# Attention with q/k pieces made a turn earlier, the output weights loaded behind the last transpose, and VectorE's low half behind its maximum

## The chip, the cores and the metric

The kernel runs on one core of a Trainium2 chip. The metric is device time of one launch in microseconds. Five engines matter: TensorE (PE, matmuls into PSUM), VectorE (DVE), ScalarE (ACT), GpSimd (POOL) and SyncE (SP, which here only issues DMAs). They run side by side, each in the order of its own program, and wait for each other by semaphores.

## The reference, cut to what matters

The program has two layers, each an attention times a gate from a mixture of experts. The change touches only the first layer's attention, over 1024 tokens of width 256, with 16 heads of 128:

```python
q = jnp.einsum('bse,ehd->bshd', x, wq)
k = jnp.einsum('bse,ehd->bshd', x, wk)
v = jnp.einsum('bse,ehd->bshd', x, wv)
qn = rms_norm(q, q_scale)
kn = rms_norm(k, k_scale)
scores = jnp.einsum('bqhd,bkhd->bhqk', qn, kn)
attn = jax.nn.softmax(scores, axis=-1)
out = jnp.einsum('bhqk,bkhd->bqhd', attn, v)
return jnp.einsum('bqhd,hde->bqe', out, wo)
```

## The kernel before

A turn t is one head; in it stand eight steps m, one for each tile of 128 queries against all 1024 keys. Every matmul operand is kept as a high and a low f16 half, so each product is three matmuls. The order on every engine is written out by hand; there is no scheduler.

One tile goes through these instructions. TensorE makes its scores into two of four PSUM banks (L1102 to L1106). VectorE takes the negated row maximum from PSUM (`a_nmax`, L1237). ScalarE takes the exponential into one of two buffers `a_ex`, with the row sum in an accumulator that a second instruction reads out (L1180). VectorE makes the scale of the rows from the sum (`a_part`, `a_share`, L1241 and L1243; called share here). ScalarE writes the scaled high half (`a_halves`, L934), VectorE the low half (L940). SP transposes both by DMA (L949) into `a_pT`, and TensorE multiplies with v (L1118 to L1120, called values). There are three `a_halves` buffers, so a high half also waits for the transpose three tiles back.

The waits of the exponential decide much here. `exps(t, m)` waits for its maximum and for the low half of tile m - 2, which is the last reader of the buffer that it writes:

```python
u, past = (t, m - 2) if m >= 2 else (t - 1, QT + m - 2)
wait_low(act, u, past)
```

In step m, TensorE makes the scores of tile m + 2, a side piece, and a quarter of the values. ScalarE takes the exponential of tile m + 1, copies the side pieces out of PSUM, and writes the high half of tile m + 1. VectorE's step is: low half of tile m, share of m + 1, maximum of m + 2, side work.

The ten side pieces prepare the coming heads. Pieces 0 to 3 are q and k (two token tiles each, L1088 to L1090; ScalarE copies out the squares, L1159, and the value, L1160), 4 and 5 are v (ScalarE's high half L1171, VectorE's low half L1230), 6 to 9 are transposes of the normalised q and k (L1075, ScalarE L1166, VectorE L1225). They take turns in two PSUM banks, so that a piece waits until the piece two before it is copied out, with its low half where it has one. `MADE` says which piece of which head stands in which step. Between q/k and their transposes stands the norm, in two halves: VectorE sums the squares (`squares`, L1210 and L1213), GpSimd takes the power (L1026) and multiplies q and k (L1029). GpSimd also splits the weights of coming heads (L712 to L716) and weights of later stages (L801 to L805).

At the end, `wo_halves` (two tiles of 1 MB that lie over `sq` and `qk`) are loaded, and the next stage's `project` (L1857 to L1859) multiplies the heads' outputs with them, head by head.

Of the kernel before, what the change touches and what calls it, by code (L numbers as in the profile page):

```python
# [16 lines left out]
D = 256  # L17
# [6 lines left out]
H, HD = 16, 128  # L24
# [790 lines left out]
def attention0(nc, env, w):  # L815

    sem, psum, ident = env["sem"], env["psum"], env["ident"]
# [2 lines left out]
            ("turn", 0, 0), ("turn", 1, 0), ("turn", 0, 1), ("turn", 1, 1)]  # L820
    NS, QK, TURN_FIRST = len(SIDE), 4, 6

    MADE = {0: (1, (3,)), 1: (1, (6,)), 2: (1, (7, 4)), 3: (1, (8,)), 4: (1, (9, 5)),
            5: (2, (0,)), 6: (2, (1,)), 7: (2, (2,))}
    VALUES = {5: (0, 0, 0), 6: (0, 0, 1), 7: (0, 0, 2), 0: (1, 0, 3), 1: (1, 1, 0), 2: (1, 1, 1), 3: (1, 1, 2), 4: (1, 1, 3)}
    OUT_AT = {2: 0, 6: 1}
    VB, PB = 3, 3
# [9 lines left out]
    def coming(t, ahead):  # L837

        return not fixed(t) or t + ahead < H

    FIRST = [("side", 0, s) for s in range(NS)] + [("side", 1, s) for s in range(3)]

    def units(t):

        if fixed(t) and t < 0:
            return FIRST
        made = []
        for m in range(QT):
            ahead, sides = MADE[m]
            if coming(t, ahead):  # L850
                made += [("side", ahead, s) for s in sides]
        return made

    def has_low(unit):
# [18 lines left out]
    def unit_count(t, unit):  # L873
        return first_unit(t) + units(t).index(unit) + 1
# [9 lines left out]
    with ExitStack() as local:  # L884
# [9 lines left out]
        later = SplitWeights(nc, env, w, tmp)  # L894
# [4 lines left out]
        total, part, share = (tmp(n, [P, QT]) for n in ("total", "part", "share"))  # L899
# [2 lines left out]
        halves = [tmp(f"halves{b}", [P, KT, 2, P], F16) for b in range(PB)]  # L902

        scale_loaded = [sem(f"a0_sld{b}") for b in range(2)]
        wo_loaded = sem("a0_wol")
        turned = [sem(f"a0_tu{b}") for b in range(PB)]
        (scale_ready, made, high_done, low_done, ss_ready, var_ready, pow_ready, r_ready, qkn_ready, s_ready, max_ready,
         exp_ready, part_ready, share_ready, p_high, p_low, pv_ready, o_high, o_low) = (
# [9 lines left out]
            return psum[:, at:at + 2, :].rearrange("p a b -> p (a b)")  # L918

        def sides_at(t, m):  # L920
            ahead, sides = MADE[m]
            return [("side", ahead, s) for s in sides] if coming(t, ahead) else []

        def wait_low(engine, t, m):

# [11 lines left out]
        def tile_low(dve, t, m):  # L937
            i = QT * t + m
            dve.wait_ge(p_high, i + 1)
            dve.scalar_tensor_tensor(halves[i % PB][:, :, 1, :], ex[m % 2][:, :].rearrange("p (k q) -> p k q", q=P),  # L940
                                     share[:, m:m + 1], halves[i % PB][:, :, 0, :], ALU.mult, ALU.subtract).then_inc(p_low, 1)
# [33 lines left out]
        with nc.Block() as block:  # L975
            @block.sync
            def _(sp):
                def load(h):
                    sp.wait_ge(w_ready, h - 1)
                    weights.load(sp, h, h % 2)  # L980

                for i, name in enumerate(("L0_attn_q_scale", "L0_attn_k_scale")):
                    sp.dma_start(scales[:, i:i + 1], w[name].rearrange("(p a) -> p a", a=1)).then_inc(scale_loaded[i], 16)
                load(2)
                for k in range(2):
                    later.load(sp, k)
                for t in range(H):
                    turn_tile(sp, t, 0)
                    if t + 3 < H:
                        load(t + 3)  # L990
                    turn_tile(sp, t, 1)
                    if t > 0:
                        later.store(sp, t - 1)
                    if 0 < t < later.CHUNKS - 1:
                        later.load(sp, t + 1)
                    turn_tile(sp, t, 2)
                    if t == H - 1:
                        sp.wait_ge(ss_ready, 2 * H)
                        sp.wait_ge(made, unit_count(H - 2, ("side", 1, NS - 1)))
                        later.wait_stored(sp, later.WO_CHUNKS)  # L1000
                        for part, dst in enumerate(env["wo_halves"]):
                            sp.dma_start(dst.rearrange("p h e -> p (h e)"), env["split_rest"][:, part, 0:H * D])\
                              .then_inc(wo_loaded, 16)
                    for m in range(3, QT):
                        turn_tile(sp, t, m)
                sp.wait_ge(wo_loaded, 32)

            @block.gpsimd
            def _(pool):
                pool.memset(power[:, :], -0.5).then_inc(pow_ready, 1)  # L1010
                pool.wait_ge(scale_loaded[0], 16)
                pool.wait_ge(scale_loaded[1], 16)

                pool.tensor_tensor(qk_scale[:, 0:1], scales[:, 0:1], scales[:, 1:2], ALU.mult).then_inc(scale_ready, 1)
                pool.memset(qk_scale[:, 1:2], 1.0).then_inc(scale_ready, 1)
                pool.wait_ge(pow_ready, 1)

                def split_weights(t, b, loads, users):

                    pool.wait_ge(made, users)  # L1020
                    weights.split(pool, t, b, loads)

                def normalise(t, half):
                    cols, tiles = slice(half * NT, (half + 1) * NT), slice(half * NT // 2, (half + 1) * NT // 2)
                    pool.wait_ge(var_ready, 2 * t + half + 1)
                    pool.tensor_tensor(rnorm[:, cols], ss[:, cols], power[:, cols], ALU.pow).then_inc(r_ready, 1)  # L1026
                    pool.wait_ge(r_ready, 2 * t + half + 1)
                    flat = qk[:, tiles, :, :].rearrange("p n j d -> p (n j) d")
                    pool.tensor_tensor(flat, flat, bcast(rnorm[:, cols], 2, HD), ALU.mult).then_inc(qkn_ready, 1)  # L1029

                last_v = ("side", 1, TURN_FIRST - 1)
                for half in range(2):
                    normalise(0, half)
                split_weights(2, 0, 2, TURN_FIRST)
                for t in range(H):
                    if t + 1 < H:
                        for half in range(2):
                            normalise(t + 1, half)
                    if t < later.CHUNKS:
                        later.split(pool, t)  # L1040
                    if t + 3 < H:
                        split_weights(t + 3, (t + 3) % 2, (t + 3) // 2 + 1, unit_count(t, last_v))

            @block.tensor
            def _(pe):
# [158 lines left out]
            def _(dve):  # L1204
# [27 lines left out]
                def maxima(t, m):  # L1232
                    k = m % 2
                    dve.wait_ge(s_ready, QT * t + m + 1)
                    if not (fixed(t) and t == 0 and m < 2):
                        dve.wait_ge(exp_ready, QT * t + m - 1)
                    dve.tensor_reduce(nmax[:, k:k + 1], score_banks(m), AX.X, ALU.max, negate=True).then_inc(max_ready, 1)  # L1237
# [6 lines left out]

                def head(t, r):
                    for m in range(QT):
                        tile_low(dve, t, m)
                        if m < QT - 1:
                            shares(t, m + 1)
                        elif coming(t, 1):  # L1250
                            shares(t + 1, 0)
                        if m < QT - 2:
                            maxima(t, m + 2)
                        elif coming(t, 1):
                            maxima(t + 1, m + 2 - QT)
                        for unit in sides_at(t, m):
                            if has_low(unit):
                                side(t, unit, r)
                        if m == 1 and coming(t, 1):
                            squares(t + 1, 1, unit_count(t, ("side", 1, 3)))  # L1260
                        if m == 7 and coming(t, 2):
                            squares(t + 2, 0, unit_count(t, ("side", 2, 1)))
                        if m - 1 in OUT_AT and t > 0:
                            low_outputs(dve, t - 1, OUT_AT[m - 1])
# [433 lines left out]
def gated_linear_attention(nc, env, w, out):  # L1698
# [114 lines left out]
    with nc.Block() as block:  # L1813
# [34 lines left out]
        def _(pe):  # L1848
            def project(n):
                if n >= 4:  # L1850
                    pe.wait_ge(gated_ready, n - 3)
                out = psum[:, n % 4, 0:D]
                for h in range(H):
                    oh, ol = (o[:, h, n * P:(n + 1) * P] for o in (oT_h, oT_l))
                    if n == NT // 2 and h == H - 1:
                        pe.wait_ge(o_low, o_count)
                    pe.matmul(out, oh, wo_h[:, h, :], start=(h == 0), stop=False)  # L1857
                    pe.matmul(out, oh, wo_l[:, h, :], start=False, stop=False)
                    last = pe.matmul(out, ol, wo_h[:, h, :], start=False, stop=(h == H - 1))  # L1859
                last.then_inc(y_ready, 1)  # L1860
# [829 lines left out]
```

## Time and profile before

| what | us |
|---|---|
| median of 3 runs | 1079.27 (1079.18 to 1079.59) |
| the profiled execution | 1080.21, span 1078.4 |
| first to last exponential (L1180) | 165.1 to 675.6 |
| busy over the span: PE, DVE, ACT, POOL | 947.4, 806.0, 630.9, 484.2 |

The profiled execution is one launch; its span is from its first instruction to its last. Busy time is the time in which an engine works on an instruction, matmul ends being modelled. The attention of the first layer takes nearly half of the span; what follows it is not touched.

### The profile page before, as it was taken

What the parts mean: (1) busy time and instruction counts of PE and PEld (TensorE: products, weight loads), DVE (VectorE), ACT (ScalarE), POOL (GpSimd) and SP (SyncE); (2) the same over time, 40 slices, a digit from 0 to 9 for tenths busy, and PEclk for the clock granted to TensorE, in tenths of its full rate; (3) what the DMA queues carried; (4) which work ended last, traced back from release to release, by engine and by line L of the source; (5) the groups of instructions that cost most, each with busy time, mean ns of one, the idle gap of its engine ahead of it and who ended that gap; (6) DMA issues with size and microseconds to landing.
All of it is one profiled execution on the core that took longest, in us unless ns stands there. A gap on an engine that the chain in (4) does not pass through costs nothing. (4 is left out here: it accounts for less than half of the span.)

```text
span 1078.4 us, 18348 instructions
## 1 busy us (share of the span) xinstructions
PE 947.4 (88%) x6414; PEld 592.2 (55%) x6414; DVE 806.0 (75%) x1445; ACT 630.9 (58%) x1097; POOL 484.2 (45%) x385
## 2 busy tenths in 40 slices
PE   5976977999999999999999997899697789799797
PEld 4455754565555565555555552596243456577444
DVE  3958438999999999999999998255899537364267
ACT  3646037887888887888887887235210337446341
POOL 3130645556665556665556450200681027432273
PEclk9985988999999999999999999899899889799899
DMA  5475115788989889889879879501122266578632
GB/s 173 106 194 168 29 45 100 158 150 165 179 170 172 157 155 169 177 167 165 165 153 176 158 137 234 111 1 60 58 79 97 87 193 202 164 228 280 207 98 84
DMA packets 380881, 155.61 MB, mean 144 GB/s; under 512 B 287556, under 2 KB 378230, under 8 KB 380534
## 3 DMA queue, kind: packets, MB, share of 16 engines
q1 hardware_dynamic: 363286, 131.23, 56.1%
q10 hardware_dynamic: 14432, 14.81, 4.1%
q0 software_dynamic: 3072, 8.39, 2.3%
q8 instruction: 52, 0.85, 0.3%
q14 instruction: 39, 0.32, 0.1%
HBM read 60.93 MB, written 23.72 MB: 78 GB/s over the span
## 5 line engine op out<-in xcount | busy, mean ns | idle before, releaser
L940 DVE SCALAR_TENSOR_TENSOR a_halves<-a_ex,a_share,a_halves 128x1024 f16<-128x1024 f32 x128 | 190.5, 1488 | 36.9 <-ACT a_halves L934 34.9
L1237 DVE TENSOR_REDUCE a_nmax<-psum 128x1 f32<-128x1024 f32 x128 | 156.5, 1223 | 6.6 <-PE psum L1106 6.3
L1026 POOL TENSOR_TENSOR a_rnorm<-a_ss,a_power 128x8 f32<-128x8 f32 x32 | 67.9, 2121 | 194.1 <-DVE a_ss L1213 194.0
L934 ACT ACTIVATE a_halves<-a_ex,a_share 128x1024 f16<-128x1024 f32 x128 | 146.8, 1147 | 12.8 <-DVE a_share L1243 7.2
L1180 ACT ACTIVATE a_ex<-psum,a_nmax 128x1024 f32<-128x1024 f32 x128 | 142.6, 1114 | 0.5 <-DVE a_nmax L1237 0.5
L1088 PE MATMUL psum<-a_wh,xT_h 128*128 128x128 f16 (+1 forms) x512 | 115.8, 248 | 4.3 <-PEq L2657 2.0
L1089 PE MATMUL psum<-a_wl,xT_h 128*128 128x128 f16 (+1 forms) x512 | 115.6, 248 | 0.0
L1090 PE MATMUL psum<-a_wh,xT_l 128*128 128x128 f16 (+1 forms) x512 | 115.6, 248 | 0.0
L1118 PE MATMUL psum<-a_pT,a_vh 128*128 128x512 f16 x256 | 98.7, 385 | 10.5 <-DMA a_pT<-a_halves 10.5
L1120 PE MATMUL psum<-a_pT,a_vl 128*128 128x512 f16 x256 | 98.5, 385 | 0.0
L1119 PE MATMUL psum<-a_pT,a_vh 128*128 128x512 f16 x256 | 98.4, 384 | 0.0
L1102 PE MATMUL psum<-a_qkTh 128*128 128x512 f16 x256 | 76.7, 381 | 2.8 <-ACT a_ex L1180 2.8
L1693 DVE TENSOR_TENSOR g_e_hf<-psum,g_e_sg 64x128 f32<-64x128 f32 x96 | 28.2, 294 | 64.9 <-ACT g_e_sg L1659 58.4
L1104 PE MATMUL psum<-a_qkTl,a_qkTh 128*128 128x512 f16 x256 | 76.6, 381 | 0.0
L1106 PE MATMUL psum<-a_qkTh,a_qkTl 128*128 128x512 f16 x256 | 76.6, 381 | 0.0
L1618 POOL COPY g_e_gu<-g_e_raw 128x256 f32<-128x256 f32 x96 | 38.9, 438 | 78.0 <-DMA g_e_raw<-in_L_ffn_wu 62.6
L1807 POOL DMA_INDIRECT sorted_tokens<-g_xn,g_r_slot x32 | 42.5, 1328 | 69.6 <-DVE g_r_slot L1394 60.1
L1075 PE MATMUL psum<-ident,qk 128*128 128x128 f32 x256 | 40.9, 286 | 31.6 <-POOL qk L1029 28.5
L1159 ACT ACTIVATE sq<-psum 128x512 f32<-128x512 f32 x64 | 38.2, 597 | 45.3 <-PE psum L1090 45.3
L1166 ACT ACTIVATE a_qkTh<-psum,a_qk_scale 128x512 f16<-128x512 f32 x64 | 43.9, 687 | 33.3 <-PE psum L1075 29.1
L1029 POOL TENSOR_TENSOR qk<-qk,a_rnorm 128x1024 f32<-128x1024 f32 x32 | 61.5, 1921 | 2.5
L1639 PE MATMUL psum<-g_xTs,g_e_gu 128*128 x384 | 56.8, 297 | 5.2 <-POOL g_e_gu L1618 5.2
(389 smaller groups left out, 2409.2 us busy)
## 6 DMA issues: line engine op xcount, KB each, us to landing
block_outputs<-g_e_ym ACTq DMA_DIRECT2D x16, 512.0 KB, 3.6
split_rest<-a_e_wh SPq DMA_DIRECT2D x15, 384.0 KB, 3.2
wf<-in_L_ffn_W_gate SPq DMA_DIRECT2D x32, 128.0 KB, 2.6
wf<-in_L_ffn_W_up SPq DMA_DIRECT2D x32, 128.0 KB, 2.6
wf<-in_L_ffn_W_down SPq DMA_DIRECT2D x32, 128.0 KB, 3.0
g_rows<-sorted_tokens SPq DMA_DIRECT2D x16, 256.0 KB, 4.3
g_e_raw<-in_L_ffn_wg SPq DMA_DIRECT2D x32, 128.0 KB, 3.1
g_e_raw<-in_L_ffn_wu SPq DMA_DIRECT2D x32, 128.0 KB, 3.4
```

The source lines that it names most:

```text
L934: act.activation(halves[i % PB][:, :, 0, :], ex[m % 2][:, :].rearrange("p (k q) -> p k q", q=P), ACT.Copy, scale=share[:, m:m + 1]).then_i ...
L940: dve.scalar_tensor_tensor(halves[i % PB][:, :, 1, :], ex[m % 2][:, :].rearrange("p (k q) -> p k q", q=P), share[:, m:m + 1], halves[i % P ...
L1088: pe.matmul(dst, xh, wh, start=(c == 0), stop=False)
L1089: pe.matmul(dst, xh, wl, start=False, stop=False)
L1090: last = pe.matmul(dst, xl, wh, start=False, stop=(c == DC - 1))
L1102: pe.matmul(psum[:, bank + f, :], qh, kh[f], start=True, stop=False)
L1104: pe.matmul(psum[:, bank + f, :], qh, kl[f], start=False, stop=False)
L1118: pe.matmul(out, vh[:, k, :], ph, start=(k == 0), stop=False)
L1119: pe.matmul(out, vh[:, k, :], pl, start=False, stop=False)
L1120: last = pe.matmul(out, vl[:, k, :], ph, start=False, stop=(k == KT - 1))
L1180: act.activation(ex[m % 2][:, :], score_banks(m), ACT.Exp, bias=nmax[:, m % 2:m % 2 + 1], accum_out=total[:, m:m + 1]).then_inc(exp_ready, 1)
L1237: dve.tensor_reduce(nmax[:, k:k + 1], score_banks(m), AX.X, ALU.max, negate=True).then_inc(max_ready, 1)
```

## The change

Four things are changed. (1) Piece 3 of a head is made two turns ahead like pieces 0 to 2: the v pieces move to steps 0 and 2, and the q/k pieces stand in steps 4 to 7 of one turn. The prologue makes one piece more for head 1. (2) VectorE's sums of squares stand in step 0 (half 1) and step 6 (half 0) instead of 1 and 7, and GpSimd's norm of half 0 moves to the end of the turn before. (3) In VectorE's step the low half stands behind the share and the maximum. (4) The output weights are loaded behind the last transpose in four pieces of four heads, with a semaphore each, and TensorE's projection waits for each piece.

```diff
-    MADE = {0: (1, (3,)), 1: (1, (6,)), 2: (1, (7, 4)), 3: (1, (8,)), 4: (1, (9, 5)),
-            5: (2, (0,)), 6: (2, (1,)), 7: (2, (2,))}
+    MADE = {0: ((1, 4),), 1: ((1, 6),), 2: ((1, 7), (1, 5)), 3: ((1, 8),), 4: ((1, 9), (2, 0)), 5: ((2, 1),), 6: ((2, 2),),
+            7: ((2, 3),)}
...
-    FIRST = [("side", 0, s) for s in range(NS)] + [("side", 1, s) for s in range(3)]
+    FIRST = [("side", 0, s) for s in range(NS)] + [("side", 1, s) for s in range(QK)]
...
-        wo_loaded = sem("a0_wol")
+        env["wo_loaded"] = [sem(f"a0_wol{i}") for i in range(4)]
...
                     turn_tile(sp, t, 2)
-                    if t == H - 1:
-                        sp.wait_ge(ss_ready, 2 * H)
-                        sp.wait_ge(made, unit_count(H - 2, ("side", 1, NS - 1)))
-                        later.wait_stored(sp, later.WO_CHUNKS)
-                        for part, dst in enumerate(env["wo_halves"]):
-                            sp.dma_start(dst.rearrange("p h e -> p (h e)"), env["split_rest"][:, part, 0:H * D])\
-                              .then_inc(wo_loaded, 16)
                     for m in range(3, QT):
                         turn_tile(sp, t, m)
-                sp.wait_ge(wo_loaded, 32)
+                sp.wait_ge(ss_ready, 2 * H)
+                sp.wait_ge(made, unit_count(H - 2, ("side", 1, NS - 1)))
+                later.wait_stored(sp, later.WO_CHUNKS)
+                for i, loaded in enumerate(env["wo_loaded"]):
+                    four = slice(4 * i, 4 * i + 4)
+                    for part, dst in enumerate(env["wo_halves"]):
+                        sp.dma_start(dst[:, four, :].rearrange("p h e -> p (h e)"),
+                                     env["split_rest"][:, part, 4 * i * D:4 * (i + 1) * D]).then_inc(loaded, 16)
...
                 split_weights(2, 0, 2, TURN_FIRST)
+                normalise(1, 0)
                 for t in range(H):
                     if t + 1 < H:
-                        for half in range(2):
-                            normalise(t + 1, half)
+                        normalise(t + 1, 1)
                     if t < later.CHUNKS:
                         later.split(pool, t)
                     if t + 3 < H:
                         split_weights(t + 3, (t + 3) % 2, (t + 3) // 2 + 1, unit_count(t, last_v))
+                    if t + 2 < H:
+                        normalise(t + 2, 0)
...
                 def head(t, r):
                     for m in range(QT):
-                        tile_low(dve, t, m)
                         if m < QT - 1:
                             shares(t, m + 1)
                         elif coming(t, 1):
@@ -1253,12 +1251,13 @@
                             maxima(t, m + 2)
                         elif coming(t, 1):
                             maxima(t + 1, m + 2 - QT)
+                        tile_low(dve, t, m)
                         for unit in sides_at(t, m):
                             if has_low(unit):
                                 side(t, unit, r)
-                        if m == 1 and coming(t, 1):
-                            squares(t + 1, 1, unit_count(t, ("side", 1, 3)))
-                        if m == 7 and coming(t, 2):
+                        if m == 0 and coming(t, 1):
+                            squares(t + 1, 1, unit_count(t - 1, ("side", 2, QK - 1)) if t else len(FIRST))
+                        if m == 6 and coming(t, 2):
                             squares(t + 2, 0, unit_count(t, ("side", 2, 1)))
...
                 for h in range(H):
                     oh, ol = (o[:, h, n * P:(n + 1) * P] for o in (oT_h, oT_l))
+                    if n == 0 and h % 4 == 0:
+                        pe.wait_ge(env["wo_loaded"][h // 4], 32)
```

On VectorE, steps 6 and 7 of a turn read like this before. The rows with `a0_halves` are the low halves (of tiles 6 and 7, from the exponential buffers `a0_ex0` and `a0_ex1`), `a0_part` and `a0_share` the share of the next tile, `a0_nmax` the maximum two tiles on, `a0_ss` the squares and `oT_l` the low half of an output:

```order
L940 SCALAR_TENSOR_TENSOR a0_halves1<-a0_ex0,a0_share,a0_halves1 128x8x128
L1241 TENSOR_SCALAR a0_part<-a0_total 128x1
L1243 RECIPROCAL a0_share<-a0_part 128x1
L1237 TENSOR_REDUCE a0_nmax<-psum 128x1
L940 SCALAR_TENSOR_TENSOR a0_halves2<-a0_ex1,a0_share,a0_halves2 128x8x128
L1241 TENSOR_SCALAR a0_part<-a0_total 128x1
L1243 RECIPROCAL a0_share<-a0_part 128x1
L1237 TENSOR_REDUCE a0_nmax<-psum 128x1
L1210 TENSOR_REDUCE a0_ss<-sq 128x8
L1213 TENSOR_SCALAR a0_ss<-a0_ss 128x8
L963 SCALAR_TENSOR_TENSOR oT_l<-psum,oT_h 128x512
```

And the same two steps after (line numbers are three or one lower there):

```order
L1240 TENSOR_SCALAR a0_part<-a0_total 128x1
L1242 RECIPROCAL a0_share<-a0_part 128x1
L1236 TENSOR_REDUCE a0_nmax<-psum 128x1
L937 SCALAR_TENSOR_TENSOR a0_halves2<-a0_ex0,a0_share,a0_halves2 128x8x128
L1209 TENSOR_REDUCE a0_ss<-sq 128x8
L1212 TENSOR_SCALAR a0_ss<-a0_ss 128x8
L1240 TENSOR_SCALAR a0_part<-a0_total 128x1
L1242 RECIPROCAL a0_share<-a0_part 128x1
L1236 TENSOR_REDUCE a0_nmax<-psum 128x1
L937 SCALAR_TENSOR_TENSOR a0_halves0<-a0_ex1,a0_share,a0_halves0 128x8x128
L960 SCALAR_TENSOR_TENSOR oT_l<-psum,oT_h 128x512
```

The low half moved behind share and maximum of its step, so that the next instruction but the sides is the share of the tile that reuses its buffer; the squares moved a step ahead.

On SP, the end of the attention before: the transposes of a turn's tiles (`a_pT`), the store of the last split chunk, and the two loads of the output weights (into `sq` and `qk`):

```order
L949 DMA_TRANSPOSE a_pT<-a_halves 128x16x128 x8
L809 DMA split_rest<-a_e_wh 256x1x768
L949 DMA_TRANSPOSE a_pT<-a_halves 128x16x128
L1002 DMA sq<-split_rest 128x4096
L1002 DMA qk<-split_rest 128x4096
L949 DMA_TRANSPOSE a_pT<-a_halves 128x16x128 x5
```

And after:

```order
L946 DMA_TRANSPOSE a_pT<-a_halves 128x16x128 x8
L809 DMA split_rest<-a_e_wh 256x1x768
L946 DMA_TRANSPOSE a_pT<-a_halves 128x16x128 x6
L1002 DMA sq<-split_rest 128x1024
L1002 DMA qk<-split_rest 128x1024
L1002 DMA sq<-split_rest 128x1024
L1002 DMA qk<-split_rest 128x1024
L1002 DMA sq<-split_rest 128x1024
L1002 DMA qk<-split_rest 128x1024
L1002 DMA sq<-split_rest 128x1024
L1002 DMA qk<-split_rest 128x1024
```

The loads moved past the last five transposes and became eight.

## Rows read from the trace of the kernel before

**Rows 1.** Busy us by stretch: PE, PEld, DVE, ACT, POOL, PEclk, DMA share, GB/s.

```profile
400.00:500.00 100.00, 94.84 (x639) 56.73 (x637) 92.97 (x137) 82.31 (x125) 59.44 (x31) 1.00 0.88 166
```

**Rows 2.** Waits between 160 and 700: us in all, times, longest.

```profile
PE psum L1075 <- POOL qk L1029: 26.6, 17, 3.3
```

**Rows 3.** Timeline of GpSimd and TensorE: start us, us, engine, line, operation, [idle before].

```profile
398.76 1.90 POOL L1029 TENSOR_TENSOR qk<-qk,a_rnorm 128x1024 f32<-128x1024 f32 x1
...
407.89 1.90 POOL L1029 TENSOR_TENSOR qk<-qk,a_rnorm 128x1024 f32<-128x1024 f32 x1
...
409.93 0.63 PE L1075 MATMUL psum<-ident,qk 128*128 128x128 f32 x4 [1.54 <-POOL qk L1029]
```

**Rows 4.** Timeline of VectorE in one turn.

```profile
388.57 1.94 DVE L940 SCALAR_TENSOR_TENSOR a_halves<-a_ex,a_share,a_halves 128x1024 f16<-128x1024 f32 x1 [0.79 <-ACT a_halves L934]
...
400.27 1.47 DVE L940 SCALAR_TENSOR_TENSOR a_halves<-a_ex,a_share,a_halves 128x1024 f16<-128x1024 f32 x1
...
403.72 1.21 DVE L1210 TENSOR_REDUCE a_ss<-sq 128x8 f32<-128x1024 f32 x1
...
405.04 1.28 DVE L940 SCALAR_TENSOR_TENSOR a_halves<-a_ex,a_share,a_halves 128x1024 f16<-128x1024 f32 x1
406.24 0.14 DVE L1241 TENSOR_SCALAR a_part<-a_total 128x1 f32<-128x1 f32 x1
...
406.50 1.22 DVE L1237 TENSOR_REDUCE a_nmax<-psum 128x1 f32<-128x1024 f32 x1
407.63 0.74 DVE L1225 SCALAR_TENSOR_TENSOR a_qkTl<-psum,a_qk_scale,a_qkTh 128x512 f16<-128x512 f32 x1
...
408.89 1.97 DVE L940 SCALAR_TENSOR_TENSOR a_halves<-a_ex,a_share,a_halves 128x1024 f16<-128x1024 f32 x1
...
421.01 1.94 DVE L940 SCALAR_TENSOR_TENSOR a_halves<-a_ex,a_share,a_halves 128x1024 f16<-128x1024 f32 x1 [0.79 <-ACT a_halves L934]
```

**Rows 5.** Timeline of ScalarE and VectorE in turn 15.

```profile
661.87 1.11 ACT L1180 ACTIVATE a_ex<-psum,a_nmax 128x1024 f32<-128x1024 f32 x1
...
662.88 0.19 ACT L1180 ACTIVATION_READ_ACCUMULATOR a_ex<-psum,a_nmax 128x1 f32 x1
...
663.30 0.16 DVE L1243 RECIPROCAL a_share<-a_part 128x1 f32<-128x1 f32 x1
...
663.50 1.15 ACT L934 ACTIVATE a_halves<-a_ex,a_share 128x1024 f16<-128x1024 f32 x1 [0.42 <-DVE a_share L1243]
```

**Rows 6.** Timeline of ScalarE in a step 2.

```profile
404.19 0.19 ACT L1180 ACTIVATION_READ_ACCUMULATOR a_ex<-psum,a_nmax 128x1 f32 x1
...
405.84 0.60 ACT L1171 ACTIVATE a_vh<-psum 128x512 f16<-128x512 f32 x1 [0.65 <-PE psum L1090]
...
407.85 1.12 ACT L1180 ACTIVATE a_ex<-psum,a_nmax 128x1024 f32<-128x1024 f32 x1
```

**Rows 7.** VectorE's groups, 200 to 700: busy us, mean ns, idle before.

```profile
L940 DVE SCALAR_TENSOR_TENSOR a_halves<-a_ex,a_share,a_halves 128x1024 f16<-128x1024 f32 x120 | 177.6, 1480 | 34.4 <-ACT a_halves L934 32.4
```

**Rows 8.** Timeline, first low halves of turns 14 and 15, ScalarE's wait, last low half.

```profile
625.01 1.28 DVE L940 SCALAR_TENSOR_TENSOR a_halves<-a_ex,a_share,a_halves 128x1024 f16<-128x1024 f32 x1
...
653.64 1.27 DVE L940 SCALAR_TENSOR_TENSOR a_halves<-a_ex,a_share,a_halves 128x1024 f16<-128x1024 f32 x1
...
674.51 1.15 ACT L934 ACTIVATE a_halves<-a_ex,a_share 128x1024 f16<-128x1024 f32 x1 [5.48 <-DMA a_pT<-a_halves]
...
678.46 1.28 DVE L940 SCALAR_TENSOR_TENSOR a_halves<-a_ex,a_share,a_halves 128x1024 f16<-128x1024 f32 x1 [1.22 <-ACT a_halves L934]
```

**Rows 9.** DMA issues: KB, us from issue to landing.

```profile
qk<-split_rest SPq DMA_DIRECT2D x1, 1024.0 KB, 7.7
```

**Rows 10.** Timeline of TensorE: a q/k piece starts, the values behind it start.

```profile
388.81 0.27 PE L1088 MATMUL psum<-a_wh,xT_h 128*128 128x256 f16 x1
...
390.12 0.38 PE L1118 MATMUL psum<-a_pT,a_vh 128*128 128x512 f16 x1
```

**Rows 11.** Busy us by stretch in turn 0, columns as in rows 1.

```profile
180.00:185.00 5.00, 3.29 (x10) 1.83 (x11) 4.97 (x8) 2.90 (x5) 4.92 (x3) 0.56 0.66 125
```

More of the change, by code:

```diff
@@ L848, in units @@
         for m in range(QT):
-            ahead, sides = MADE[m]
-            if coming(t, ahead):
-                made += [("side", ahead, s) for s in sides]
+            made += [("side", ahead, s) for ahead, s in MADE[m] if coming(t, ahead)]
         return made
@@ L920, in sides_at @@
         def sides_at(t, m):
-            ahead, sides = MADE[m]
-            return [("side", ahead, s) for s in sides] if coming(t, ahead) else []
+            return [("side", ahead, s) for ahead, s in MADE[m] if coming(t, ahead)]
         def wait_low(engine, t, m):
```

## The prediction

> **What bounds the kernel now.** I read the busy times by stretch first, then the waits, then the timeline of one turn engine by engine. In the attention stage (span 165 to 680) TensorE is busy 94.84 of 100 us and VectorE 92.97 [rows 1], both close to full; a turn takes 421.01 - 388.57 = 32.44 us, low half to same low half [rows 4]. So a turn is worth reading instruction by instruction. TensorE has one stall worth the name: it waits for GpSimd's norm, 26.6 us in 17 waits [rows 2]. In the turn at 400 the norm's product starts at 407.89, ends at 409.79, and the transpose of q/k goes at 409.93 after 1.54 idle [rows 3]. VectorE waits 34.4 us in all before its low halves, mostly for ScalarE's high half [rows 7], which is late because ScalarE waits for TensorE's pieces. So before, TensorE with its wait for the norm sets the pace and VectorE, nearly as full, follows.
>
> Per tile VectorE runs low half, share, maximum. I call them L(m), S(m+1), M(m+2) in step m, and ScalarE's work E(m) (exponential) and H(m) (high half).
>
> **Part 1, q/k pieces and norm a turn ahead.** The sum over 16 turns keeps every instruction; one q/k piece moves to the prologue. In each turn squares for half 0 now come in step 6 and for half 1 in step 0, so GpSimd's pow and product end a step or more before TensorE's transposes in steps 1 and 3. GpSimd itself now waits for squares last in its turn; behind that stands only the next turn's half 1, not due before TensorE's step 3. The wait of [rows 2] goes: at most -26.6 us, if nothing else takes its place.
>
> **Part 2, L behind M.** This one adds a wait that no diff line shows. E(m+1) writes the buffer that L(m-1) reads (two ex buffers), and L1180 waits for that. Before, VectorE passed from L(m-1) to S(m+1) by way of M(m+1), its sides and L(m), so E(m+1) ran beside those. After, VectorE's order is S(m), M(m+1), L(m-1), sides, S(m+1): between L(m-1) and S(m+1) only the sides are left, and S(m+1) needs E(m+1). Behind the waiting S stand M and the next L, and for these wait ScalarE, TensorE's scores two tiles on, and SP's transposes. The step is thus a closed ring:
> L 1.28 (405.04) [rows 4]; handover 0.04 (663.30 + 0.16 to 663.50); E to the end of its accumulator read, 661.87 to 663.07, 1.20; handover 0.04 [rows 5]; S 406.50 - 406.24 = 0.26; M 407.63 - 406.50 = 1.13 [rows 4]. Sum 3.95, eight of them 31.6 us a turn, a floor that no other engine's haste can lower. Without E and its handovers VectorE's three take 2.6.
>
> What comes on top of the floor:
> - Sides. VectorE's next slot opens 1.20 after L starts (406.24 - 405.04), S can start 2.56 after it, so the gap is 1.36. Two sides take 1.26 (407.63 to 408.89), so 0.63 each; squares with their scaling 405.04 - 403.72 = 1.32 [rows 4]. Only step 0 (v's low half and squares, 1.95) overflows: +0.59.
> - Late pieces. In steps 2, 4 and 6 ScalarE has two or three sides before H, and the second piece in a PSUM bank now waits for a low half that VectorE makes after L. Before, step 2 took 407.85 - (404.19 + 0.19) = 3.47 from read to next E with a piece late by 0.65 [rows 6]; after, L ends 2.75 past the read (handover, 0.26, 1.13, 1.28, handover), so such a step costs up to 0.72. Bounds 0 and 3 x 0.72 = 2.2; I take 0.3 each, 0.9, as the pieces are late by less than a copy.
> - L against GpSimd. Mean L is 1480 ns against 1.28 undisturbed [rows 4, 7]: 8 x 0.20 = 1.6 a turn. GpSimd keeps its ten operations a turn, L its eight. In the ring each such loss lengthens the turn in full. Bounds 0 and 8 x 0.69 = 5.5 (the worst row, 1.97 at 408.89); I take the mean, 1.6.
>
> On that last term two rows say more. L at 408.89 began 0.90 before the product ended and took 0.69 longer; L at 400.27 began 0.39 before and took 0.19 longer [rows 3, 4]. The Trainium skill, "SBUF — State Buffer", section "SBUF: two separate sides", says that GpSimd and a VectorE operation with two SBUF inputs take a port pair by exclusive lock and the loser blocks for the whole instruction. Both rows agree (the rest of the operation less 0.2). By the mean the term is 1.6 a turn; by that rule it hangs on where GpSimd's operations fall, which is a rival below.
>
> Turn 1 to 13, and 0 alike: 31.6 + 0.59 + 0.9 + 1.6 = 34.7 against 32.44, +2.25, times 14 = +31.5. Turn 14 has no q/k pieces for a head 16 and half of the GpSimd work: 31.6 + 0.59 + 0.3 + 0.8 = 33.3 against 653.64 - 625.01 = 28.6 [rows 8], +4.7.
>
> **Part 3, the output weights.** In turn 15 SP put two 1 MB loads ahead of five transposes, and ScalarE waited 5.48 for a buffer that a transpose had to free (674.51) [rows 8]. That stall goes. But turn 15 has hardly any sides to hide E: L(0) to L(7) took 678.46 - 653.64 = 24.8 with the stall; now six rings of 3.95 and 0.6 for the last tile, which has no M, 24.3: -0.5. SP issues eight loads behind the last transpose; queued past them is only the next stage's loading. The projection's first four heads need the first pair. It starts only after the last tile's transpose has landed and TensorE has made the last head's values; that covers the loads, as the slower whole megabyte landed in 7.7 [rows 9]. If the cover went, I bound the wait at those 7.7; I take 0.
>
> **Prologue.** One more q/k piece before the first scores: 390.12 - 388.81 = 1.3 on TensorE [rows 10], with nothing beside it. Bounds 0 and twice that at half clock.
>
> **Sum.** +31.5 + 4.7 - 0.5 + 1.3 = +37.0 on the profiled execution's 1080.2 (span 1078.4), 1117.2. The median of the runs is 0.9 below that execution: 1116.3.
>
> **Rivals.**
> - Ring without additions (same). If pieces are in time and L meets nothing: 32.2 a turn, -0.25 x 14, turn 14 +3.6, -0.5, +1.3: +0.9, so 1080.2 in the median. For it: sides fill the gaps almost exactly. Against: the losses of L are in the trace before. 0.05.
> - Faster. The norm's wait is what pays, and E's exposure is filled: it decides if the gap between L and S falls below the sides' mean, 7.7 / 8 = 0.96, where VectorE's work and TensorE's decide again. Then -26.6 - 5.5 + 1.3 gives 1048.5. For it: two engines above 92 %. Against: E alone is 1.20 [rows 5] and nothing shortens it. 0.04.
> - L blocked for whole operations. Twice a turn L could start with a 1.90 product and lose 1.7 each time instead of 0.69: +2.0 a turn, +28, 1144. For it: both rows above; against: in the ring an operation that L blocks starts behind L, so the two may well take turns. 0.10. The Trainium skill's lock rule ("SBUF — State Buffer", the section above) is this case, and would give its 1144 where the mean gives 1116.
> - Half clock. In turn 0 at 180 to 185 TensorE, busy 3.29 of 5, had granted clock 0.56 [rows 11], and the level below 2.4 is 1.2 GHz. In turn 15 and the end of 14 a step has only scores and values, each with as many columns as a q/k piece (1.3, [rows 10]): 2.6 of 3.95, as thin. At 1.2 GHz it needs 5.2: 11 steps x 1.25 = +14, 1130. Against: in turns 1 to 13 TensorE still works 30 of 35. 0.07.
>
> **How the numbers follow.** Forecast 0.74, rivals 0.05, 0.04, 0.10, 0.07. The forecast's own spread goes from half the additions (1095) to double lateness and L losses half as large again (about 1140). I give 1095 to 1136: inside are some 0.70 of the forecast, the half clock and part of the lock case; outside the two on the other side, most of the lock case and a tail. A difference of 0.2 % (2 us) is what a measurement of this kernel can tell. Faster 0.04, same 0.05, slower 0.91.
>
> **What would show it.** In the profile after: VectorE idle before S (L1240) with ScalarE's exponential as releaser, about 1 us in each step with few sides, and idle before L gone; E waiting for L; TensorE's wait for the product gone; turns of 34 to 35.5; ScalarE's 5.48 wait near the end gone and none on the output weights. It would be wrong if E starts before L(m-1) ends, or if turns are near 30.

## The result and the profile after

The changed kernel takes 1125.06 us in the median of four runs (1122.22 to 1127.89), the kernel before 1079.22: a ratio of 1.0429 (95 % interval 1.0405 to 1.0454). Its profiled execution, the fastest of the four, took 1122.22 with a span of 1120.5, 42.1 more than the span before.

Every engine is less busy in the middle of the kernel. The window of [rows 1], columns as there:

```profile
400.00:500.00 100.00, 90.45 (x607) 53.03 (x606) 86.55 (x127) 76.50 (x118) 56.27 (x29) 1.00 0.79 154
```

So no engine is filled; the added time is waiting. The waits of the changed kernel from 160 to 740 (us in all, times, longest) show where:

```profile
ACT a_ex L1179 <- DVE a_halves L937: 99.2, 72, 2.4
DVE a_part L1240 <- ACT a_ex L1179: 73.9, 93, 2.3
...
PE psum L1087 <- DVE a_qkTl L1224: 37.3, 30, 2.0
...
PE psum L1101 <- ACT a_ex L1179: 15.7, 19, 2.1
```

ScalarE's exponential waits for VectorE's low half, and VectorE's share for the exponential: each engine waits for the other, in turns. TensorE's wait for the norm product, 26.6 in [rows 2], has no row any more; in its place TensorE waits for VectorE's side work (L1087) and for the exponential (L1101).

One step without side work on VectorE, in turn 15, first VectorE and then ScalarE (start us, us, engine, line, operation, [idle before]); it answers to [rows 4, 5]:

```profile
703.55 1.28 DVE L937 SCALAR_TENSOR_TENSOR a_halves<-a_ex,a_share,a_halves 128x1024 f16<-128x1024 f32 x1
706.16 0.15 DVE L1240 TENSOR_SCALAR a_part<-a_total 128x1 f32<-128x1 f32 x1 [1.33 <-ACT a_ex L1179]
706.35 0.17 DVE L1242 RECIPROCAL a_share<-a_part 128x1 f32<-128x1 f32 x1
706.43 1.22 DVE L1236 TENSOR_REDUCE a_nmax<-psum 128x1 f32<-128x1024 f32 x1
707.58 1.27 DVE L937 SCALAR_TENSOR_TENSOR a_halves<-a_ex,a_share,a_halves 128x1024 f16<-128x1024 f32 x1
```

```profile
704.92 1.11 ACT L1179 ACTIVATE a_ex<-psum,a_nmax 128x1024 f32<-128x1024 f32 x1 [1.25 <-DVE a_halves L937]
705.94 0.19 ACT L1179 ACTIVATION_READ_ACCUMULATOR a_ex<-psum,a_nmax 128x1 f32 x1
```

Read it round, in the prediction's letters (L low half, E exponential, S share, M maximum): L starts at 703.55, E 1.37 later, S 1.24 after that, M 0.27 after S, the next L 1.15 after M. That is the ring: 4.03 here, and 4.02 in step 1 of every one of turns 1 to 13. The prediction had 3.95.

Where the 42.1 went, from the start of L in each turn: first L at 173.33 for 169.13 (+4.2); turns 0 to 13 492.1 for 455.9 (+36.3), turn 14 34.1 for 28.6 (+5.4); turn 15 24.2 for 24.8 (-0.6); from there to the projection's first matmul +0.8; from that to the end 382.4 for 386.4 (-4.0, in stages that the change doesn't touch).

These last 4.0 go with the granted clock of the one execution, not with the change. The same 1912 matmuls ran there at another clock (the column behind GpSimd's, 0.92 and 0.95; first the kernel before, then the changed one, from the projection's first matmul to the end):

```profile
692.01:1078.40 386.39, 335.36 (x1912) 215.03 (x1912) 238.73 (x473) 143.04 (x314) 143.22 (x193) 0.92 0.42 131
```

```profile
738.08:1120.50 382.42, 329.76 (x1912) 211.69 (x1912) 239.39 (x473) 142.96 (x314) 142.51 (x193) 0.95 0.42 132
```

Over all twelve traces of this case that stretch takes 379.4 (at 0.96) to 390.5 (at 0.92), whatever the kernel. Up to the projection the change costs 46.1 (738.08 for 692.01).

The end of the attention, TensorE's first value product that waited for the last transposes and the projection's first matmul:

```profile
730.91 0.58 PE L1117 MATMUL psum<-a_pT,a_vh 128*128 128x512 f16 x1 [8.08 <-DMA a_pT<-a_halves]
...
738.08 0.27 PE L1858 MATMUL psum<-sq,oT_h 128*128 128x256 f16 x1 [0.32 <-PEq L972]
```

No row waits for the output weights, though SP issued the first load only at 728.52, and the 5.48 of [rows 8] is gone.

Turns 1 to 13 are not alike (33.3 to 36.5). Here are the two kinds of tile 7: VectorE's low half, then GpSimd's norm product.

```profile
414.30 2.99 DVE L937 SCALAR_TENSOR_TENSOR a_halves<-a_ex,a_share,a_halves 128x1024 f16<-128x1024 f32 x1
...
449.32 1.27 DVE L937 SCALAR_TENSOR_TENSOR a_halves<-a_ex,a_share,a_halves 128x1024 f16<-128x1024 f32 x1
```

```profile
414.31 1.90 POOL L1026 TENSOR_TENSOR qk<-qk,a_rnorm 128x1024 f32<-128x1024 f32 x1
...
449.44 2.91 POOL L1026 TENSOR_TENSOR qk<-qk,a_rnorm 128x1024 f32<-128x1024 f32 x1
```

They start within 0.01 of each other at 414.3, and L takes 1.71 more than alone; with a lead of 0.12, at 449.3, L loses nothing and the product takes 1.01 more. In 9 of turns 1 to 13 L lost 1.71 there, with a recorded lead of 0.01 or 0.02; in 4, with a lead of 0.12 to 0.39, nothing.

### The profile page after: what moved, and what is told of

It reads as the page before. It is cut to its first block and busy times, and to the rows that moved or that the text cites. A ratio compares the mean times of both kernels' runs of the same rounds, so it can differ in the third digit from the quotient of the medians.

```text
span 1120.5 us, 18353 instructions
## 1 busy us (share of the span) xinstructions
PE 948.4 (85%) x6414; PEld 585.7 (52%) x6414; DVE 812.1 (72%) x1445; ACT 629.7 (56%) x1097; POOL 480.6 (43%) x385
## 5 line engine op out<-in xcount | busy, mean ns | idle before, releaser
L1179 ACT ACTIVATE a_ex<-psum,a_nmax 128x1024 f32<-128x1024 f32 x128 | 142.8, 1116 | 99.6 <-DVE a_halves L937 99.2
L1087 PE MATMUL psum<-a_wh,xT_h 128*128 128x128 f16 (+1 forms) x512 | 116.4, 250 | 40.7 <-DVE a_qkTl L1224 38.0
L1023 POOL TENSOR_TENSOR a_rnorm<-a_ss,a_power 128x8 f32<-128x8 f32 x32 | 52.4, 1639 | 175.2 <-DVE a_ss L1212 175.1
L1101 PE MATMUL psum<-a_qkTh 128*128 128x512 f16 x256 | 76.8, 382 | 15.7 <-ACT a_ex L1179 15.7
L1087 PEld LDWEIGHTS psum<-a_wh,xT_h 128*128 128x128 f16 x512 | 50.5, 99 | 63.4 <-DVE a_qkTl L1224 52.7
L1026 POOL TENSOR_TENSOR qk<-qk,a_rnorm 128x1024 f32<-128x1024 f32 x32 | 74.4, 2326 | 2.5
L1240 DVE TENSOR_SCALAR a_part<-a_total 128x1 f32<-128x1 f32 x128 | 19.6, 153 | 75.0 <-ACT a_ex L1179 73.9
L1806 POOL DMA_INDIRECT sorted_tokens<-g_xn,g_r_slot x32 | 40.2, 1257 | 69.6 <-DVE g_r_slot L1393 60.1
```

The costliest lines, as they stand in the source:

```text
L1087: pe.matmul(dst, xh, wh, start=(c == 0), stop=False)
L1101: pe.matmul(psum[:, bank + f, :], qh, kh[f], start=True, stop=False)
L1179: act.activation(ex[m % 2][:, :], score_banks(m), ACT.Exp, bias=nmax[:, m % 2:m % 2 + 1], accum_out=total[:, m:m + 1]).then_inc(exp_ready, 1)
```

## The experiments

Ratios are to the kernel before, timed beside each. "Before" and "changed" are the two kernels; the three parts are the earlier pieces and norm, L behind M, and the later output weights.

**1. Changed, with L first again.**

```diff
+                        tile_low(dve, t, m)
                         if m < QT - 1:
                             shares(t, m + 1)
...
-                        tile_low(dve, t, m)
```

> The changed kernel with VectorE's order put back: the low half L(m) first in a step, then shares S(m+1) and maximum M(m+2); the earlier q/k pieces and norm and the later output weights stay. Ring theory: the closed ring L, E, S, M is gone, and so is TensorE's wait for the norm product (26.6 us before). Turns of 30 to 31, VectorE's idle time before S falls below 15 us in all, total 1045 to 1062. Rival (the earlier pieces and norm cost what was lost): turns stay at 34 to 36, total 1105 or more. Second rival (the norm's wait is replaced by another of the same size): 1072 to 1082.

Measured: 1084.52, ratio 1.0046 (1.0013 to 1.0079). The order of VectorE alone is worth 40 of the changed kernel's 46. But the gain that I expected beside it did not come. Window and VectorE's group of L (200 to 640: busy us, mean ns, idle before):

```profile
400.00:500.00 100.00, 93.14 (x624) 54.87 (x622) 96.84 (x133) 80.30 (x120) 62.02 (x31) 1.00 0.84 163
```

```profile
L937 DVE SCALAR_TENSOR_TENSOR a_halves<-a_ex,a_share,a_halves 128x1024 f16<-128x1024 f32 x106 | 185.9, 1753 | 10.4 <-ACT a_halves L931 9.5
```

VectorE is now nearly full, because L takes 1753 ns in the mean, where the kernel before has 1501 in the same window (1480 in the longer one of [rows 7]). L loses 3.9 a turn in the mean of turns 1 to 13, before 1.8. Squares in steps 0 and 6 let GpSimd start its product just ahead of an L, as here (L, then the product):

```profile
402.81 2.63 DVE L937 SCALAR_TENSOR_TENSOR a_halves<-a_ex,a_share,a_halves 128x1024 f16<-128x1024 f32 x1
```

```profile
402.47 1.90 POOL L1026 TENSOR_TENSOR qk<-qk,a_rnorm 128x1024 f32<-128x1024 f32 x1
```

So the norm's wait (0.6 is left of it) was replaced by another of about the same size: TensorE waits 25.6 for VectorE's side work (L1087). That is the second rival, though the time lies 2.5 above its range; the mechanism was one I had priced only inside the ring.

**2. Before, with L behind M and nothing else.**

```diff
-                        tile_low(dve, t, m)
                         if m < QT - 1:
                             shares(t, m + 1)
...
+                        tile_low(dve, t, m)
```

> The kernel before with VectorE's order alone changed: L(m) behind M(m+2); pieces, norm and output weights as before. Ring theory: turns of 34.5 to 36 whatever the pieces do, the wait for the norm product hidden in the ring, and the stall of turn 15 (5.5) stays, total 1112 to 1132. Rival (the order alone is harmless): 1075 to 1085.

Measured: 1135.16, ratio 1.0514 (1.0469 to 1.0558), 3 above the range, with turns of 34.3 to 37.5. Waits from 160 to 740:

```profile
ACT a_ex L1180 <- DVE a_halves L940: 82.2, 75, 2.8
DVE a_part L1241 <- ACT a_ex L1180: 81.9, 57, 3.2
PE psum L1075 <- POOL qk L1029: 45.8, 29, 3.1
```

The order makes the ring by itself. One point failed: the norm's wait is not hidden but grows from 26.6 to 45.8, and on top of the ring the two other parts together save 10 (1135.16 to 1125.06).

**3. Before, with the output weights behind the last transpose.**

```diff
-                    if t == H - 1:
-                        sp.wait_ge(ss_ready, 2 * H)
...
+                for i, loaded in enumerate(env["wo_loaded"]):
```

> The kernel before with the output weights alone moved behind the last transpose, in four pairs of loads. Theory: ScalarE's wait of 5.48 in turn 15 goes, what is late next takes back up to half of it, and TensorE waits nothing for the weights: 1074 to 1077. Rival: the loads then end later than the last values, and TensorE waits for them up to 7.7: 1079 to 1083.

Measured: 1075.15, ratio 0.9978 (0.9953 to 1.0003): about what was expected, but not told apart from no change. In its trace the last low half starts 19.8 after that of tile 0 in turn 15, before 24.8, so 5.0 are saved. From there to the projection's first matmul it takes 14.2 for 13.6, so 0.6 is given back: TensorE waits 4.94 instead of 2.47 for the last transposes and then makes its first values slower (0.58 each for 0.38, at a granted clock of 0.50 from 680 to 682). The projection starts 3.8 earlier (688.26 for 692.01); that gain is a reading of two single executions.

**4. Changed, with three buffers for the exponentials.**

```diff
-        ex = [tmp(f"ex{b}", [P, T]) for b in range(2)]
+        ex = [tmp(f"ex{b}", [P, T]) for b in range(EB)]
...
-                        wait_low(act, u, past)
+                    if i >= EB:
+                        act.wait_ge(p_low, i - EB + 1)
```

> The changed kernel with three buffers for the exponentials instead of two, L still behind M. To make room, GpSimd's split of the later weights has one load buffer instead of two, and its load is issued at the end of a turn. Ring theory: E(m+1) waits for L(m-2) only, so the ring is open: ScalarE's wait for L and VectorE's idle time before S fall to less than a third, turns of 30.5 to 32.5, total 1045 to 1075. Rival (VectorE's losses against GpSimd, or the late pieces, set the turn): turns stay above 34, total 1105 or more.

Measured: 1097.07, ratio 1.0188 (1.0123 to 1.0252): between the two ranges. ScalarE's wait for L, 99.2 in the changed kernel, has no row left, so the ring is open, and 28 of the 46 come back. Not all of that is the ring: L loses 1.24 a turn here for 1.92 in the changed kernel, 10 in 14 turns. (What the single load buffer does by itself was not run.) VectorE still waits for the exponential, 55.1 in all. ScalarE in a step 2 shows one reason:

```profile
413.99 0.60 ACT L1169 ACTIVATE a_vh<-psum 128x512 f16<-128x512 f32 x1 [1.62 <-PE psum L1088]
414.49 0.59 ACT L955 ACTIVATE oT_h<-psum 128x512 f16<-128x512 f32 x1
414.96 1.15 ACT L931 ACTIVATE a_halves<-a_ex,a_share 128x1024 f16<-128x1024 f32 x1
416.00 1.11 ACT L1177 ACTIVATE a_ex<-psum,a_nmax 128x1024 f32<-128x1024 f32 x1
```

A late piece (v) holds ScalarE for 1.62, and the high half and the next exponential stand behind it. Its turns are 32.65 where L loses next to nothing, up to 35.45 where it loses 3.1.

**5. Changed, with the norm product in four.**

```diff
-                    pool.tensor_tensor(flat, flat, bcast(rnorm[:, cols], 2, HD), ALU.mult).then_inc(qkn_ready, 1)
+                    for q in range(4):
...
+                        pool.tensor_tensor(flat[:, two, :], flat[:, two, :], bcast(rnorm[:, at], 2, HD), ALU.mult)\
+                            .then_inc(qkn_ready, 1)
```

> The changed kernel with GpSimd's norm product cut into four operations of a quarter each (1.90 in all before); everything else stays. Lock theory (L waits for the rest of the GpSimd operation that came first): the loss of 1.71 at tile 7 becomes at most one quarter, 0.5, and the turn, a closed ring, gets shorter by about 0.9 in the mean: 1105 to 1115. Rival (L and GpSimd share a bandwidth, so that L loses by the time beside each other): the loss stays above 1.2 and the total within 1119 to 1131.

Measured: 1116.81, ratio 1.0341 (1.0285 to 1.0397), 2 above the range. At tile 7 L loses 0.43 where it lost 1.71, in 9 of 13 turns as in the changed kernel: the wait is for the rest of one operation. L loses 0.81 a turn less in the mean, and the turn is 0.83 shorter (34.48 for 35.31): in the ring a loss of L counts in full. The first L starts 2.3 later in this execution, which is more than the time is above the range.

**6. Experiment 1, with all of GpSimd's products and weight splits in four.**

```diff
+        for c in parts:
+            pool.tensor_tensor(high[:, c], flat[:, c], lift[:, c], ALU.mult).then_inc(self.w_high, 1)
...
```

> The changed kernel with VectorE's low half first again (as in the first experiment, 1084.5) and with GpSimd's norm products and weight splits all cut into four. Lock theory: the losses of L, 3.2 to 4.9 a turn there, fall below 2, the turn goes from 33.2 to 31 or less, total 1045 to 1065. Rival (shared bandwidth, or TensorE's own work decides): turns stay at 32 to 34, 1075 or more.

Measured: 1063.73, ratio 0.9844 (0.9789 to 0.9898): faster than both kernels. Window, and L's group (200 to 640):

```profile
400.00:500.00 100.00, 97.48 (x670) 58.91 (x669) 93.55 (x143) 83.98 (x127) 81.91 (x107) 1.00 0.93 172
```

```profile
L950 DVE SCALAR_TENSOR_TENSOR a_halves<-a_ex,a_share,a_halves 128x1024 f16<-128x1024 f32 x112 | 152.1, 1358 | 28.1 <-ACT a_halves L944 26.3
```

L loses 0.7 a turn, and TensorE is 97.48 of 100 busy. The turn is 31.7 in the mean of turns 1 to 13, where 31 or less was expected; that TensorE's own work now sets it is read from its busy time, no run tests it.

**7. Experiment 3, with the same cut.** The diff is that of experiment 6.

> The kernel before with the output weights behind the last transpose (as in the third experiment, 1075) and with GpSimd's norm products and weight splits cut into four. Lock theory: L's losses, 1.8 a turn, fall to about 1, and turns from 32.44 to about 31.5; the norm's wait of 1.9 stays: 1058 to 1068. Rival (TensorE's chain with the norm's wait sets the turn, not L): turns stay at 32.3 to 32.6, 1072 to 1078.

Measured: 1110.99, ratio 1.0270 (1.0202 to 1.0338). Both theories missed, in sign. L loses hardly 0.2 a turn, but nine of turns 1 to 13 take 34.4 and four 35.4 to 36.1. TensorE's wait in all, and the product of which it waits for the end:

```profile
PE psum L1091 <- POOL qk L1044: 55.5, 29, 4.7
```

```profile
415.09 3.31 POOL L1044 TENSOR_TENSOR qk<-qk,a_rnorm 128x256 f32<-128x256 f32 x4
```

```profile
418.55 0.63 PE L1091 MATMUL psum<-ident,qk 128*128 128x128 f32 x4 [1.55 <-POOL qk L1044]
```

What L no longer loses GpSimd does: the product takes 3.31 in four for 1.90 in one, and without the earlier norm TensorE waits for its end. The cutting alone is 0.43 of these 1.41 (four quarters took 2.33 at 150.82, before the first L); the rest is waiting for L. With the earlier norm (experiment 6) TensorE's wait for it is 1.0 in all. So part 1 is worth 47 us as soon as GpSimd gives way, and costs 9 where it does not (1075.15 to 1084.52).

**8. Changed, with a copy of 256 columns more ahead of each exponential.**

```diff
+                    act.activation(extra[:, :], xT_h[:, 0, 0:256], ACT.Copy)
                     act.activation(ex[m % 2][:, :], score_banks(m), ACT.Exp, ...
```

> The changed kernel with a copy of 256 columns more on ScalarE right before each exponential, some 0.25 by half of the copies of 512 columns (0.49 from start to start). ScalarE is busy 76 of 100 there. Ring theory: each copy stands between L and E, so a turn gets longer by eight times 0.25, 2.0, in 16 turns 30: 1145 to 1165. Rival (the turn is set elsewhere and ScalarE has room): 1120 to 1132.

Measured: 1152.60, ratio 1.0666 (1.0607 to 1.0725). The copy puts E 0.32 later, and the bare step (one without side work) goes from 4.02 to 4.32, on an engine that was busy 76.50 of 100. Where the gap was filled already it adds nothing: step 0 stays at 4.52, and a turn grows by 1.5 in the mean (36.8 for 35.3), not by eight times 0.3. The rows show a bare step:

```profile
729.90 0.42 ACT L1180 ACTIVATE a_extra<-xT_h 128x256 f16<-128x256 f16 x1 [1.24 <-DVE a_halves L938]
730.22 1.10 ACT L1181 ACTIVATE a_ex<-psum,a_nmax 128x1024 f32<-128x1024 f32 x1
```

**9. Changed, with the cut of experiment 6.**

> The changed kernel, with its order (L behind M), and GpSimd's norm products and weight splits cut into four. With L first this made 1063.7 of 1084.5. Ring theory: the losses of L fall below 0.6 a turn as there, but the ring of 4.02 a step stays, with 0.5 in step 0 and about 0.9 of late pieces: turns of 33.3 to 34, total 1095 to 1110. Rival (the changed kernel lost to GpSimd alone, and the order costs nothing without it): turns below 32.5, total 1060 to 1075.

Measured: 1105.11, ratio 1.0275 (1.0223 to 1.0326), turns 0 to 13 of 33.4 to 34.9, step 1 still 4.02. The order costs 41 beside experiment 6, where L loses as much (0.7 a turn for 0.6), so these 41 are the ring's. Without the cut it was 40, but that near agreement is chance: there L lost 1.9 a turn in the ring and 3.9 with L first. In the ring the cut takes 1.3 of loss and 1.5 of turn, with L first 3.2 of loss and the same 1.5 of turn.

**10. Experiment 4, with the cut.**

> The kernel with three buffers for the exponentials (1097, one load buffer for the later weights), and GpSimd's norm products and weight splits cut into four. Undisturbed turns were 32.65 there and the mean 33.5. Theory: the rest above the kernel with L first comes half from L's losses, half from late q/k pieces that stand between two exponentials on ScalarE; the cut takes the losses alone: turns of 32.3 to 32.8, total 1078 to 1092. Rival (all of the rest is L's losses): turns of 31.8 or less, 1060 to 1075.

Measured: 1086.53, ratio 1.0083 (1.0055 to 1.0110), turns 1 to 13 of 32.6 to 33.2, the top a little over the forecast. L loses 0.6 a turn, as in experiment 9, and the two differ by 19 in time: that is what the third buffer (with the single load buffer) is worth at equal losses. The cut gave 10. The turn is still 1.1 longer than in experiment 6, and step 2, in which the late v piece stands, takes 4.95 for 3.87 there, which is that much.

## Why the prediction was right, step by step

The sum gave 1116.3 (range 1095 to 1136), the median of the runs is 1125.06, and the mechanism that the prediction names is the one that the runs show.

**The ring** was the cause: the order alone makes it (2), a third buffer opens it (4), work put into it lengthens each bare step by as much (8). Its size was 0.07 too small, 8 x 0.07 = 0.6 a turn: E starts 0.09 after L's end where I took 0.04 from the one behind the short reciprocal, and M to L is 1.15 for 1.13. (VectorE's three without E make 2.67 by the prediction's own terms, not 2.6; nothing hangs on it.)

**Additions.** Step 0 overflowed by 0.50 (0.59). L against GpSimd took 1.9 a turn (1.6). Late pieces are what is left, 0.7 (0.9), and half of it stands in step 6 (4.39 where L loses nothing). So turns 1 to 13 are 35.3 in the mean for 34.7. The sum took every turn before as 32.44; turns 0 to 13 were 455.9 together, 1.7 more than 14 of those, which hid part of the shortfall.

**L against GpSimd** was right near the mean, and partly by luck, for a reason that the mean does not show. The norm's product at tile 7 took 1.2 of the 1.9; GpSimd's other operations took 0.7, mostly at tile 3. Either operation waits for nearly the whole rest of the other (414.3 and 449.3 above, and 0.43 in experiment 5). That agrees with the Trainium skill, "SBUF — State Buffer", section "SBUF: two separate sides", on the port pair that one of the two holds by exclusive lock: 1.71 of the product's 1.90. Which of the two comes first there is not the order of the recorded starts: L lost with a lead of 0.01 or 0.02. My rival with that rule had it hit twice a turn, for 2.0; the product hit once, in 9 of 13 turns, and in which ones changes with what GpSimd did before. My argument against that rival, that the two take turns, held for 4 of 13.

**The norm's wait.** "At most -26.6, if nothing else takes its place" was right, and experiment 1 shows what takes it where there is no ring: L, losing 2.1 more a turn. Had the change left VectorE's order alone, the price of at most -26.6 would have been wrong in sign (+9 from experiment 3 to 1).

**Output weights.** -0.6 in turn 15 for -0.5, and no wait for the loads, as forecast. The make-up differs: five rings of 4.02, then 2.9 and 1.3, as the last two tiles need no maximum, where the sum had six rings and 0.6.

**Prologue** was the term furthest off for its size: +4.2 for +1.3. VectorE's first maximum starts 1.7 later (165.50 for 163.81), but that is no measure of the extra piece: experiments 2 and 3, which have the prologue of the kernel before, start it at 165.81 and 165.37. So no run here tells the 1.3 apart from the spread of single executions. The other 2.5 are the ring's first step: from the first maximum to the first L it takes 7.83 (5.32 before), and the same 7.83 in experiments 2, 4 and 9, the same 5.32 in 1, 3 and 7. The first share of the ring waits 2.31 for the exponential (171.91), where before L(0) started at 169.13, ahead of that share. I had not asked what the ring does in its first step.

**Half clock** did not come in the steps of turn 15; TensorE's granted clock stayed at 1.00 with 13.55 of 20 busy and waits of up to 1.82:

```profile
700.00:720.00 20.00, 13.55 (x60) 5.59 (x61) 13.76 (x22) 12.19 (x16) 0.00 (x0) 1.00 0.74 150
```

It did come behind TensorE's wait of 8.08 for the last transposes (0.60 from 730 to 735), as in the kernel before it had come behind a wait of 7.44 in turn 15 (0.50 from 675 to 677).

The terms fell short by 8.3 (45.3 for 37.0, up to the last low half). In the profiled execution the higher clock of the later stages hid 4.0 of that. The median of the runs lies 2.8 above this execution, where the sum had put it 0.9 below, so in the median the shortfall is 8.8 again (1125.1 for 1116.3).

## What to carry to other kernels

Before an instruction is moved behind another on its engine, follow its buffer: with two buffers, a reader put behind the next tile's consumer closes a ring through the writer, and then each engine waits while none is full. Cutting a long operation on GpSimd hands its loss to the other side, so give that side slack first (experiments 6 and 7 differ in nothing else but that part of the change and make 1063.73 and 1110.99). A wait that a change removes is worth only the distance to the next one on the same engine.

## What the runs showed of the hardware

- VectorE's low half against GpSimd's products and weight splits, in the seven traces that have them all uncut: where the low half's recorded start was ahead by 0 to 0.03, it lost 1.27 to 1.73 (17 cases); ahead by 0.06 to 0.20, it lost at most 0.01 (46 cases), and GpSimd waited (1.01 more at 449.44).
- GpSimd's short power operation (128 x 8) gives way but does not block. It took 2.60 for 1.64 when it started behind an L (experiment 1, at 399.79 and 408.85). When it started first, L lost nothing (experiment 1: power from 433.46 for 1.64, L from 433.75 for 1.28), and so in every one of the 223 such meetings in the twelve traces (at most 0.02; in 61 of them the power operation had over 0.6 to go). The rule of the Trainium skill named above, by which the one that starts first holds the port pair for its whole instruction, does not show for this operation.
- The four quarters of a product took 3.31 beside an L (experiment 7) and 2.33 with none beside them, the whole one 1.90 to 2.91.
- Eight loads of 256 KB for the output weights landed 3.9 and 5.0 us after their issue (the medians of the two halves); the two 1 MB loads before had taken 5.0 and 7.7 (the longer one in [rows 9]).
